# Half of the softmax denominators are added up by POOL instead of TensorE, in a one-core attention and mixture-of-experts kernel

## The reference, cut to what matters

```python
scores = jnp.einsum('bhir,bhjr->bhij', q_lr, k_lr) * scale
scores = jnp.where(causal_mask, jnp.float32(-jnp.inf), scores)
attn = jax.nn.softmax(scores, axis=-1)
y = jnp.einsum('bhij,bhjd->bhid', attn, v)
```

## Time and profile before

| | |
|---|---|
| median of three runs | 4089.59 us |
| the profiled execution, its own time | 4093.42 us |
| span of that execution in the trace | 4091.7 us |
| TensorE busy | 3733.8 us, 91% |
| TensorE weight loads busy | 2559.5 us, 63% |
| VectorE busy | 2259.8 us, 55% |
| ScalarE busy | 1477.9 us, 36% |
| POOL busy | 660.3 us, 16% |
| mean granted clock of TensorE | 0.948 |

### The profile page before, as it was taken

The page is one execution under the profiler, slowest core; times in us unless marked ns, Lnnn a source line. Parts: engine busy times, 40 slices in busy tenths (PEclk is TensorE's granted clock), DMA queues, the critical chain, the costliest instruction groups (busy, mean ns, idle before and its releaser), DMA issues. The chain is left out here.

```text
span 4091.7 us, 57484 instructions
## 1 busy us (share of the span) xinstructions
PE 3733.8 (91%) x21481; PEld 2559.5 (63%) x21481; DVE 2259.8 (55%) x3998; ACT 1477.9 (36%) x2756; POOL 660.3 (16%) x853
## 2 busy tenths in 40 slices
PE   5899999999999999999999823799999999999995
PEld 3555555555555555555555413688888888888884
DVE  2565565664665655656646557444444444445456
ACT  1343443443443434434434401333333333333335
POOL 2021121121121211211211200011111111111113
PEclk8999999999999999999999955699999999999997
DMA  4234234143322332341332110343434434334448
GB/s 161 49 98 130 58 90 119 43 109 99 87 75 89 104 99 78 84 130 48 104 104 61 59 28 6 109 127 106 126 119 123 138 106 126 114 118 126 118 162 311
DMA packets 188919, 423.60 MB, mean 104 GB/s; under 512 B 39840, under 2 KB 42912, under 8 KB 180512
## 3 DMA queue, kind: packets, MB, share of 16 engines
q1 hardware_dynamic: 162032, 367.97, 29.3%
q0 software_dynamic: 14400, 35.14, 4.4%
q10 hardware_dynamic: 12288, 17.83, 1.5%
HBM read 246.75 MB, written 72.38 MB: 78 GB/s over the span
## 5 line engine op out<-in xcount | busy, mean ns | idle before, releaser
L849 DVE TENSOR_REDUCE max_slots<-shared_banks 128x1 f32<-128x512 f32 (+3 forms) x1536 | 768.5, 549 | 411.1 <-PE shared_banks L625 334.2
L795 ACT ACTIVATE probs<-scores_t 128x512 f32<-128x512 f32 (+3 forms) x1536 | 663.3, 497 | 672.9 <-PE scores_t L667 619.4
L1710 PE MATMUL m_ps_h<-m_tokens_t,m_w_parts 128*128 128x512 f32 x3072 | 740.6, 391 | 1.6 <-DVE m_tokens_t L1592 1.6
L1710 PE MATMUL m_ps_y<-m_w_parts,m_hidden_parts 128*128 128x512 f32 x3072 | 737.4, 390 | 0.5
L1710 PEld LDWEIGHTS m_ps_y<-m_w_parts,m_hidden_parts 128*128 128x128 f32 x3072 | 575.4, 188 | 125.7 <-issue 6.2
L1710 PEld LDWEIGHTS m_ps_h<-m_tokens_t,m_w_parts 128*128 128x128 f32 x3072 | 576.0, 188 | 120.3 <-issue 2.0
L667 PE MATMUL scores_t<-q_operands,k_operands 128*128 128x512 f32 (+3 forms) x1536 | 517.8, 395 | 40.2 <-ACT probs L795 32.2
L622 PE MATMUL shared_banks<-k_operands,q_operands 96*128 96x512 f32 (+3 forms) x1536 | 512.5, 387 | 32.9 <-DMA k_operands<-natural 12.5
L1528 ACT ACTIVATE m_hidden<-m_ps_h,m_b 128x512 f32<-128x512 f32 x256 | 176.6, 690 | 792.1 <-PE m_ps_h L1710 778.9
L527 POOL TENSOR_SCALAR_AFFINE_SELECT probs<-probs 128x256 f32<-128x256 f32 x512 | 218.9, 430 | 1425.3 <-ACT probs L795 1422.3
L622 PEld LDWEIGHTS shared_banks<-k_operands,q_operands 96*128 96x128 f32 x1536 | 296.3, 195 | 215.0 <-issue 140.5
(11 more groups left out here) (218 smaller groups left out, 3135.3 us busy)
## 6 DMA issues: line engine op xcount, KB each, us to landing
m_w_raw<-in_w1T SPq DMA_DIRECT2D x64, 1024.0 KB, 5.1
m_w_raw<-in_w2T SPq DMA_DIRECT2D x64, 1024.0 KB, 7.4
q_operands<-natural SPq DMA_DIRECT2D x384, 128.0 KB, 2.5
k_operands<-natural SPq DMA_DIRECT2D x384, 128.0 KB, 2.5
wqk_group<-scratch_wqk SPq DMA_DIRECT2D x32, 1024.0 KB, 5.3
natural<-in_xT SPq DMA_DIRECT2D x8, 2048.0 KB, 9.5
x_residual<-in_x ACTq DMA_DIRECT2D x64, 256.0 KB, 2.7
scratch_x<-probs SPq DMA_DIRECT2D x64, 256.0 KB, 2.1
```

The lines of the kernel that those rows point to most:

```text
L795: act.activation(probs[:, slot_of(k, h // 2), h % 2, c0:HALF], st[:, (HG * k + h) % SCORE_BANKS, c0:HALF], ACT.Exp, scale=SCALE).then_inc( ...
L849: dve.tensor_reduce(mx[:, h, slot:slot + 1], src[:, 0:n], AX.X, ALU.max).then_inc(bank_free[bank], 1)
L1710: mm = pe.matmul(bank, a, b, start=(first and n == 0), stop=(final and n == len(pairs) - 1))
```

## The change

- **Sums.** `weigh` for the denominators covers only columns below `UPPER` = 256 of a half; steps with `c0` of 256 or more issue none. For the upper 256 columns POOL copies (j = 0) or adds (later j) the probabilities of each pair of heads into an accumulator, one per pair (`add_probs`). At the end of each half a new item "upper" multiplies the four accumulators with ones into the upper half of `den_bank`: after part 25 for `hh` = 0, after part 2 of the next slot for `hh` = 1.
- **Waits.** `exps` also waits until POOL has added the step whose buffer it takes; "upper" waits for the last addition; the copy of j = 0 waits until "upper" has read the accumulator; VectorE drains `den_bank` at "upper". One accumulator lies in `xres`, so the second residual load moves to the start of the tail.
- **x in halves.** SyncE sends the q strips of heads 1 to 3 first, loads the first half of x, then sends the k strips of heads 1 to 3 and loads the second half. The four copies on ScalarE move to steps 4 and 6; POOL subtracts one piece (step 4), VectorE three (step 7).
- **Maxima.** Two of the early maxima move from part 9 to later parts. The reciprocals of `hh` = 1 move to parts 4 to 7 of the next slot.
- **Small exponential.** One element is exponentiated after the last square root of a batch.
- `logits` gets one buffer, `stats` two. In the experts some semaphores are merged.

```diff
-MAX_AFTER = (0, 0, 0, 0, 0, 0, 0, 0, 0, 2, 2, 1, 1, 0, 3, 0, 0, 0, 3, 0,
+MAX_AFTER = (0, 0, 0, 0, 0, 0, 0, 0, 0, 0, 2, 2, 2, 0, 3, 0, 0, 0, 3, 0,
-X_HI_AT = ((7, 0), (7, 2), (8, 0), (8, 2))
-X_LO_POOL = 2
-X_LO_AT = 6
-X_LO_DVE_AT = (8, 3)
-INVERT_AFTER = ((30, 42, 45, 45), (0, 4, 4, 5))
+X_HI_AT = ((4, 1), (4, 3), (6, 0), (6, 2))
+X_LO_POOL = 1
+X_LO_AT = 4
+X_LO_DVE_AT = (7, 0)
+INVERT_AFTER = ((30, 42, 45, 45), (4, 5, 6, 7))
+UPPER = HALF // 2
+UPPER_AFTER = (25, 2)
...
+                    if more and slot == GROUPS - AHEAD - 1:
+                        strips(b, slot, heads=(0,))
+                        g = (slot + AHEAD) % GROUPS
+                        for h in range(1, HG):
+                            strip(q_ops, Q_STRIPS, 0, g, h)
+                        n = b * GROUPS + GROUPS - 1
+                        sp.wait_ge(strips_sent[0], (n + 1) * STRIPS)
+                        for h in range(1, HG):
+                            sp.wait_ge(strips_sent[h], n * STRIPS + STRIPS // 2)
+                        load_x(b + 1, 0)
+                        for h in range(1, HG):
+                            strip(k_ops, K_STRIPS, 2, g, h)
+                        for h in range(1, HG):
+                            sp.wait_ge(strips_sent[h], (n + 1) * STRIPS)
+                        load_x(b + 1, 1)
...
+            def add_probs(b, g, k, pair):
+                hh, j, c0 = steps[k]
+                s = (b * GROUPS + g) * NE + k
+                c = max(c0, UPPER)
+                src, total = probs[:, slot_of(k, pair), :, c:HALF], acc[pair][:, :, c - UPPER:UPPER]
+                if not diagonal[k]:
+                    plain(pool, exp_done, HG * s + 2 * pair + 2 + SCORE_BANKS, pool_passed)
+                if j == 0:
+                    if pair == 0 and g == 0 and hh == 0 and b > 0:
+                        plain(pool, summed, TT * b, pool_passed)
+                    if pair == 0 and s > 0:
+                        plain(pool, den_full, 2 * (b * GROUPS + g) + hh, pool_passed)
+                    pool.tensor_copy(total, src).then_inc(added, 1)
+                else:
+                    if diagonal[k]:
+                        plain(pool, masked, (b * GROUPS + g) * N_DIAG + masked_through(k) - 1 + pair, pool_passed)
+                    plain(pool, added, 2 * (s - 1) + pair + 1, pool_passed)
+                    pool.tensor_tensor(total, total, src, ALU.add).then_inc(added, 1)
...
+                    if item[0] == "scores" and item[3] % 2 == 1:
+                        add_probs(b, item[1], item[2], item[3] // 2)
...
-                        weigh(item[2], db, lambda h, j: ones[:]).then_inc(pv_done, 1)
+                        if has_lower(item[2]):
+                            weigh(item[2], db, lambda h, j: ones[:], UPPER, 1).then_inc(pv_done, 1)
...
+            def upper(b, g, hh):
+                n = 2 * (b * GROUPS + g) + hh
+                pe.wait_ge(added, 2 * ((b * GROUPS + g) * NE + last_step(hh) + 1))
+                pe.wait_ge(den_drained, n)
+                for h in range(HG):
+                    mm = pe.matmul(db[h * DH:(h + 1) * DH, UPPER:HALF], ones[:], acc[h // 2][:, h % 2, :],
+                                   start=True, stop=True, tile_position=(0, h * DH))
+                mm.then_inc(den_full, 1)
...
+                        if item[1] == TT - 1 and b < NB - 1:
+                            act.activation(warm[:], eps[:, 0:1], ACT.Exp)
...
+                if h % 2 == 0 and s >= 2:
+                    act.wait_ge(added, 2 * (s - 2) + h // 2 + 1)
```

117 lines of the change are left out of this document (71 added, 46 removed).

## The result

The changed kernel takes 4125.2 us (median of four runs, 4118.8 to 4130.3) beside 4088.8 us for the kernel before in the same set: a ratio of 1.0082, 95% interval 1.0069 to 1.0095. It is 0.8% slower. The forecast was 3993 us with a range from 3942 to 4050, so the time fell outside it and on the other side of the kernel before. Its profiled execution has a span of 4124.2 us, 32.5 more than 4091.7.

A forecast was written before the change was run, and what follows sets the result against it. TensorE was taken to bound attention. Sums 129 us and small exponential 12 gained, less 19 for POOL's stalls and 25 for x in halves, made 97 us less: 3993 us, from 4089.6, range 3942 to 4050.

The forecast's parts named there:

- Part C: Slot 2, x in halves: excess 9.0 us instead of 5.5 in seven batches, 25 us given back.
- Part A: Attention, sums leaving TensorE: 4.05 us saved a slot over 32 slots, 129 us.
- whatever leaves TensorE's stream is worth its full time as long as no other chain ends later: Attention: the rule by which the sums taken off TensorE were credited in full, 129 us.
- Part B: Slot starts, additions on POOL: 1.1 us given back in each of 17 slots, 19 us.
- forecast stall at slot starts: Before the values of step 2, TensorE stands still 0.85 us waiting for POOL's mask, in 17 slots.
- I cost it at nothing: Slot 2: VectorE's three subtractions may hold up POOL's additions by some 4 us, made up later, so zero.
- rival 4: Attention slots: POOL becomes the bound and the kernel slower, 4420 us at twice the addition price; chance 0.05.
- The 1.5 for the clock: Slot 2: 1.5 us lost to a lower granted clock after TensorE's 5.0 us wait for strips.
- slot 2's excess of 5.5: Slot 2's second half: some 5.5 us above 37.96, laid to ScalarE's wait for x and the clock drop.
- rival 3: Slot 2 gets much worse: strips follow x, clock stays low, excess 15 instead of 9; 4035 us, chance 0.09.
- Part D: Batch start, small exponential: 1.28 us table load moves to the tail; 12 us gained over seven batches.
- Edits with one answer: Later maxima, residual load, single logits buffer and merged semaphores: worth zero.
- rival 2: Slot starts: POOL's chain is longer and the clock drops, 60 us lost instead of 19; 4034 us, chance 0.17.

The follow-up runs named there:

- strips_on_two_queues: `spread_subtraction` with head 0's three k strips issued by ScalarE in slots 1 to 3, q strips by SyncE as before; 4029.7 us.
- x_halves_only: The kernel before with only x in halves between q and k strips, at the change's places; sums stay on TensorE; 4158.9 us, ratio 1.0174.
- row_max_one_input: Changed kernel with x behind all strips at its old places, and row maxima's copy and maximum written as one-input reductions; 4041.5 us.
- strips_order_alone: Changed kernel with x's copies and subtractions at old places, both halves of x sent behind all strips, wait for q strips kept; 4087.7 us.
- x_from_scalar_queue: Changed kernel with x's copies and subtractions at old places, both halves of x issued by ScalarE on its own DMA queue; 4119.4 us.
- sums_back_on_tensore: `one_column_added` with all sums of all 512 columns back on TensorE and the "upper" groups kept; 4103.7 us.
- spread_subtraction: `masks_ahead_of_additions` with VectorE's two subtractions of x cut into four pieces at four places; 4013.3 us, ratio 0.9805.
- x_split_by_vector_alone: `spread_subtraction` with POOL's two subtractions of x given to VectorE, which does eight pieces at eight places; 4020.2 us.
- one_column_added: Changed kernel with x behind all strips at its old places, POOL adding one column per head instead of 128 or 256; 4014.1 us.
- masks_ahead_of_additions: Changed kernel with x behind all strips at old places, first maxima later, one-input row maxima, POOL masking both pairs before adding; 4019.4 us.

## Why the prediction was wrong, step by step

Three terms of the sum failed. The sums off TensorE gave some 70 us instead of 129 (90, less at least 17 for "upper"). The additions cost 46 us instead of 19, since they hold back VectorE, which was taken at nothing. Part C cost 65 us instead of 25.

**Part A, right in kind, too large.** The sums' busy time fell from 302 to 180 us, near the 170 that were to show it. The prices by start to next start were near for second halves: 3.17 us saved against 3.45, "upper" some 0.75 against 0.54. What failed is the sentence "whatever leaves TensorE's stream is worth its full time as long as no other chain ends later", which was not tried on first halves. There another chain was 0.24 us behind: six strips, issued one each 0.63 us, then landing. Of 1.73 us in an undisturbed first half 0.41 came through.

The wait of 1.1 us that replaced the sums also goes with a second loss. In the profiles of the 13 kernels with the sums gone, 84 of 264 first halves ran at a lowered granted clock, in the three with the sums on TensorE one of 62. (Counted are slots 1 to 3, without slot 3 of the last batch, and without slot 2 where it waits behind a half of x.) That took the rest: on the mean a first half gained nothing. The prediction had 0.25 us a slot for the clock; in the kernel after it is 12 us over 16 first halves. Why one half with this wait keeps its clock and another does not, no run shows.

In `strips_on_two_queues` the wait for strips is gone, and ScalarE's exponentials, held back by the three issues, end the half instead; what would end it without them is not shown. The sums were worth 90 us, of 166 by their prices, and "upper" takes back at least 17 (0.75 in each of 23 second halves).

**Part B, the stall smaller, the costly thing elsewhere.** The additions' price was right, and the forecast stall at slot starts is 0.23 us in the slot shown, not 0.85: the copy was 0.61 and not 0.7, and TensorE came later, since it had waited 1.1 us for strips. The new wait in `exps`, taken at nothing, did cost next to nothing (TensorE waited 1.6 us in all for exponentials, 430 to 2250 us). What failed is "I cost it at nothing" beside the subtraction. Additions hold VectorE back. In slot 2 a subtraction takes 2.27 us instead of 1.22 (the kernel after and `x_halves_only`), and TensorE stands still 6.0 us behind three of them instead of 2.9. At each slot's end the copy of row maxima took 1150 ns instead of 342: 0.76 us of each second half, 19 us in all, shown by `row_max_one_input`. This was read off the wrong rows: a mask of POOL held up by VectorE shows the same exclusion from POOL's side, while the side that counts is VectorE's. The prediction's rule from the Trainium skill ("SBUF — State Buffer", Who interferes with whom) names copies too, among the forms that can contend with GpSimd, and says that `tensor_reduce` on this chip never does; the traces agree, with 1150 ns and 170 ns. The prediction applied it to the two-input form alone.

In the last two slots of the last batch, where TensorE has no maxima to make, the additions did become the bound: the last three halves take 10 us more than before and go from 24.3 to 20.0 us each with one column added. This is what rival 4 describes, at the forecast price of an addition and in two slots of 32.

**Part C, right mechanism, mis-sized.** The wait for strips was forecast at 5.0 with "3 to 6" in the list of signs; it is 7.44 in the slot shown, 5.7 to 7.8 in all seven, and the half is 9 us longer. `strips_order_alone` splits it: the half grows from 15.6 to 20.2 us by the k strips' later start, and to 24.8 by x. The first term was right (3.7 to 4.7 late forecast, a wait of 3.45 measured); the second was taken at 0.8 and is 4.0 of waiting. The prediction weighed the second by the Trainium skill's order within a ring ("DMA: Bandwidth & Descriptors", Queues, rings and completion order); the lateness came, but `x_from_scalar_queue` shows that it comes from another queue too, so being behind x in the ring isn't needed for it. The same page (Issuing engines are not separate DMA queues) says that DMAs of all issuers run on the same 16 engines and interleave, and this the run bears out with 5.8 us against 1.7.

The subtraction's 2.0 us was 2.9 in `x_halves_only` and 6.0 with the additions. The 1.5 for the clock was near: the first half in the slot shown is 9.5 us longer, with 7.4 of waiting. Its source was read too mildly, since a mean of 0.53 is the lower of the two levels for nearly all of the stretch and not for about half of it.

And slot 2's excess of 5.5 wasn't the wait for x. With x in halves alone the second half was still 43.2 us, and in `sums_back_on_tensore`, where ScalarE never waits for x, it is 45.1 against 38.7 undisturbed; there TensorE waits 4.2 us behind VectorE's subtractions. Part C didn't remove the wait for x either: ScalarE waits 24.6 us in six places of the kernel after, up to 5.4, where it was 14.8, beside TensorE's wait for strips. So what part C was credited with did not exist. The mechanism was rival 3's (an excess of 15; measured 19), and the additions' hold on VectorE came on top.

**Part D, right.** The load stands in the tail, at 996.46 us in one batch, and part D gives 2.2 us a batch.

```profile
996.46 1.28 ACT L841 ACT_TABLE_LOAD   x1
```

**"Edits with one answer": zero** was too pessimistic for the tail. Together tails and first halves of slot 0 give 35 us where 21 were forecast. In each batch a wait of TensorE behind the second tile's statistics (`ln_stats`) went from 1.80 to 0.31 us, 10 us in all. Before, the residual addition of the second tile stood on POOL behind `normalise`, which waits for the reciprocals; after, POOL does it first. POOL in a tail of before, and then of after:

```profile
943.52 1.26 POOL L536 TENSOR_TENSOR y_cols<-y_cols,denominators 128x512 f32<-128x512 f32 x1 [12.63 <-DVE denominators L873]
944.74 2.49 POOL L552 TENSOR_TENSOR x_residual<-x_residual,bo_folded 128x512 f32<-128x512 f32 x2
```

```profile
950.94 1.53 POOL L611 TENSOR_TENSOR x_residual<-x_residual,bo_folded 128x512 f32<-128x512 f32 x1 [6.86 <-DMA x_residual<-in_x]
957.12 1.26 POOL L593 TENSOR_TENSOR y_cols<-y_cols,denominators 128x512 f32<-128x512 f32 x1 [4.65 <-DVE denominators L959]
```

This was read from the two timelines and not tried by itself.

**The range.** Each rival was alone in it. The time would have needed rival 3 (at 19 and not 15), a part of rival 2 (the clock did drop, in six of 16 first halves) and a mechanism that had no rival at all: that the sums' time doesn't arrive because other chains end within a fraction of a microsecond of TensorE's.

**What stays open.** 8 us of the account lie behind the last drain, some 3 of them in the last tail, 1 in the selection and 4 in the experts, and no run says why. Slot 2's second half stays 8 to 9.5 us above an undisturbed one in every repair (43.6 to 45.3), whether two long subtractions, four pieces or eight do it. The traces divide this excess: in `spread_subtraction` 4.3 of 9.1 are waits of TensorE and the rest goes with a granted clock of 0.89, in `x_split_by_vector_alone` 4.1 of 8.1, with 0.92. The place of the waits moved each time. First halves of 16.7 to 23 us are, in every kernel with the sums gone, the ones with a lowered clock; the waits in them are mostly the usual 1.1 to 1.2 us, now and then longer. In one (18.16 us, `one_column_added`) a single strip took 2.07 us to issue and TensorE waited 2.63. Why that strip was slow, and why the clock falls in some halves only, is open.

The version that beats both kernels is `spread_subtraction`, 4013.3 us, 1.95% below the kernel before; `masks_ahead_of_additions` (4019.4) can't be told from it, since their intervals overlap.

## What to carry to other kernels

Before crediting work taken off the bounding engine, list for each stretch every chain that ends within the credit (here strips 0.24 us behind) and give back what those don't yield; the credit is the smaller of the two, stretch by stretch. A wait that takes the place of removed work can also go with a lower granted clock behind it: look at the clock half by half, and not only at the waits. When an idle engine takes over work, look at what its memory accesses do to its neighbour's instructions and not only at its own queue: here 342 ns became 1150, on the critical path, 31 times. A split of a large transfer that puts small, urgent transfers beside or behind it costs their landing, whichever queue carries it.

## What the runs showed of the hardware that was not expected

- With the sums gone, TensorE waits some 1.1 us for strips in a first half, and its granted clock was below 1 in 84 of 264 first halves (0.90 where a half is 16.8 us long, 0.74 at 19.8, 0.70 at 22.8; 15.3 to 15.6 at 1.00). With the sums on TensorE it was so in one of 62.
- VectorE's copy of 128x16 float32 within SBUF takes 230 to 342 ns beside a quiet POOL and 1150 ns beside POOL's additions; the same as a reduction with one input takes 170 ns beside the additions. A subtraction of 1024 columns takes 1.22 us alone, 2.27 beside POOL's additions (the kernel after), 2.83 beside POOL's own subtractions (`one_column_added`) and 3.33 with both; POOL's addition of 512 goes from 1.29 to 1.84 and 2.24 us beside VectorE's subtractions.
- 128 KB strips land 1.7 to 1.8 us after their issue has ended, and 5.6 us after it behind a megabyte on the same queue, 5.8 beside one on another.
- An addition on POOL that reads the mask's result starts 0.28 us after the mask ends (forecast 0.15).
- Issuing one strip costs SyncE or ScalarE 0.6 us, where a residual tile cost ScalarE 0.35.
